# Moving two of nine depthwise taps onto TensorE, and the rest onto VectorE in half tiles, in the feed-forward stage of a four-layer convolution kernel

## The reference, cut to what matters

```
h   = relu(batchnorm1(c1 @ y))            384 channels, 48 x 48
g   = relu(batchnorm2(depthwise3x3(h)))   nine taps per channel, zero border
o   = c3 @ g + c3_b                       96 channels
s   = sigmoid(se2 @ relu(se1 @ mean(o)))
x   = x + o * (1 + s)
```

## Time and profile before

| | |
|---|---|
| median of 3 runs | 3150.25 us (3146.51 to 3150.44) |
| profiled execution | 3148.91 us, span of its instructions 3147.0 us |
| granted TensorE clock, mean | 0.89 of full |
| busy over the whole span | PE 2207.9 us (70%), DVE 2572.6 us (82%), ACT 1624.5 us (52%), POOL 2092.8 us (67%) |
| the changed stage, from the end of the last VectorE instruction before it to the end of its last | 2128.5 to 2322.9 us, 194.4 us |
| busy in that stretch | PE 130.29, DVE 151.95, ACT 86.20, POOL 85.14 us |

### The profile page before, as it was taken

The page is one execution under the profiler, slowest core; times in us unless marked ns, Lnnn a source line. Parts: engine busy times, 40 slices in busy tenths (PEclk is TensorE's granted clock), DMA queues, the critical chain, the costliest instruction groups (busy, mean ns, idle before and its releaser), DMA issues. The chain is left out here.

```text
span 3147.0 us, 24979 instructions
## 1 busy us (share of the span) xinstructions
PE 2207.9 (70%) x7334; PEld 1072.0 (34%) x7334; DVE 2572.6 (82%) x2080; ACT 1624.5 (52%) x2316; POOL 2092.8 (67%) x1126
## 2 busy tenths in 40 slices
PE   6754566677776676777666777789524989689389
PEld 3421233333333333333333333343112545355344
DVE  5556899999999999999999999956983656689630
ACT  2576577677677767777777677625410000263220
POOL 0154799999999999999999999933720000098000
PEclk9876799999999999999999999986666989799689
DMA  1274333333343333333343333250008888300360
GB/s 45 83 213 196 114 116 117 104 119 114 103 119 117 106 116 116 104 114 116 112 118 104 114 117 114 82 177 0 0 23 290 304 281 303 103 8 8 81 82 23
DMA packets 152198, 368.13 MB, mean 117 GB/s; under 512 B 54271, under 2 KB 69766, under 8 KB 140102
## 3 DMA queue, kind: packets, MB, share of 16 engines
q1 hardware_dynamic: 150852, 361.30, 37.3%
q10 hardware_dynamic: 1218, 5.31, 0.6%
HBM read 302.16 MB, written 51.00 MB: 112 GB/s over the span
## 5 line engine op out<-in xcount | busy, mean ns | idle before, releaser
L807 POOL TENSOR_TENSOR l0c_r<-l0c_r,l0c_v 128x768 f32<-128x768 f32 x576 | 1042.8, 1827 | 27.0 <-DVE l0c_r L770 26.5
L837 ACT ACTIVATE ps<-l0c_dlt,l0c_na 128x512 f32<-128x512 f32 (+1 forms) x1152 | 625.9, 575 | 520.0 <-DVE l0c_h L796 504.4
L816 POOL TENSOR_TENSOR l0c_hcp<-l0c_cb,l0c_h 128x768 f32<-128x768 f32 x384 | 701.9, 1828 | 1.5 <-DVE l0c_h L796 1.5
L796 DVE TENSOR_TENSOR_SCAN l0c_h<-ps,l0c_h,l0c_r 128x768 f32<-128x768 f32 x384 | 693.3, 1805 | 1.2 <-issue 1.2
L728 PE MATMUL ps<-l0c_hcp,net_ident 128*128 128x512 f32 (+1 forms) x1536 | 597.5, 514 | 14.1 <-ACT l_Z L830 7.3
L847 ACT ACTIVATE l0c_r<-l0c_S,l0c_floor,l0c_na 128x768 f32<-128x768 f32 x576 | 579.7, 1013 | 0.0
L695 PE MATMUL ps<-l0c_Bp,l0c_sel 96*128 96x512 bf16 (+1 forms) x1152 | 296.4, 340 | 381.8 <-DVE l0c_hcv L777 225.4
L770 DVE SCALAR_TENSOR_TENSOR l0c_r<-l0c_r,ps 128x768 f32<-128x768 f32 x576 | 533.8, 927 | 14.5 <-PE ps L695 9.4
L728 PEld LDWEIGHTS ps<-l0c_hcp,net_ident 128*128 128x128 f32 x1536 | 275.8, 200 | 269.4 <-issue 207.0
L1310 PE MATMUL ps<-l_prod,l_wa 128*96 128x384 f32 (+1 forms) x888 | 292.1, 493 | 85.2 <-DVE l_prod L1294 85.2
L796 DVE TENSOR_TENSOR_SCAN l0c_h<-ps,l0c_r 128x768 f32<-128x768 f32 x192 | 335.1, 1746 | 1.0
(11 more groups left out here) (274 smaller groups left out, 2530.9 us busy)
## 6 DMA issues: line engine op xcount, KB each, us to landing
l0c_cb<-cf SPq DMA_DIRECT2D x768, 192.0 KB, 3.3
l_other<-po SPq DMA_DIRECT2D x72, 1152.0 KB, 5.2
dlt<-l0s_dl SPq DMA_DIRECT2D x36, 384.0 KB, 2.3
v<-l0s_vv SPq DMA_DIRECT2D x36, 384.0 KB, 2.9
l0c_dlt<-dlt SPq DMA_DIRECT2D x36, 384.0 KB, 3.9
l0c_v<-v SPq DMA_DIRECT2D x36, 384.0 KB, 4.4
l0c_Bp<-bc SPq DMA_DIRECT2D x36, 144.0 KB, 4.0
l0c_Cp<-bc SPq DMA_DIRECT2D x36, 144.0 KB, 5.4
```

Of the source, the lines that this page charges most:

```text
L796: dve.tensor_tensor_scan(h[:, n, :], da[j % 2], r[:, j % NR, :], init, ALU.mult, ALU.add).then_inc(s_scan, 1)
L807: pool.tensor_tensor(r[:, j % NR, :], r[:, j % NR, :], v[:, (j // N) % 2, :], ALU.mult).then_inc(s_w, 1)
L816: pool.tensor_tensor(hcp[:, p % NHP, :], cb[:, p % NCB, :], h[:, e % N, :], ALU.mult).then_inc(s_hp, 1)
L837: act.activation(da[e % 2][:, part], dlt[:, i, part], ACT.Exp, scale=na[:, i, n:n + 1]).then_inc(done, 1)
```

## The change

The two sides of it are these:

- The first MM = 2 taps of every tile become products on TensorE: `diag[:, ot, i, :]` is a 128 x 128 matrix with the tap's weight of each channel on its diagonal, and the moving operand is the shifted window of `pad`. They sum in PSUM.
- The other OWN = 7 taps are all on VectorE, in half tiles of three chunks (128 x 1152). The first of the seven reads the PSUM sum as its addend, the others the accumulator.
- ScalarE's tap products and GpSimd's sums are gone. GpSimd makes the six diagonals at the start of the stage.
- The PSUM banks are dealt anew: three banks for each of two half tiles in turn (banks 0 to 5), and banks 6 and 7 in turn for all c1 and c3 chunks. The order on TensorE becomes: taps of half n, then three chunks of the next tile's c1 (for the last tile, of the first image's c3). On ScalarE: `finish` of half n - 1, then the three chunks of half n.
- `finish` and `t3` go by halves, with one `t3` buffer for each image (the first of them is the memory of Z), and c3 goes chunk by chunk for both images.
- Only the border of the `pad` buffers is cleared.

```diff
-        prod = sb("prod", [128, 2, L])
-        t3 = sb("t3", [128, OT, L])
+        acc = sb("acc", [128, 2, HB * CH])
+        diag = sb("diag", [128, OT, MM, 128])
+        t3 = (t3a, sb("t3", [128, OT, L]))
...
+            def free(r):
+
+                if r >= 2:
+                    if r - 2 < NJ * NC:
+                        pe.wait_ge(s_ev, r - 1)
+                    else:
+                        pe.wait_ge(s_o, r - 1 - NJ * NC)
+
+            def c1_chunk(j, c):
                 b, ot = tiles[j]
...
+                r = j * NC + c
+                free(r)
+                for f, (lo, hi, t) in enumerate(feeds[b]):
+                    mm = pe.matmul(ps[:, bank(6 + r % 2)], c1[lo:hi, t, ot * 128:(ot + 1) * 128],
+                                   U[lo:hi, t, c * CH:(c + 1) * CH], start=(f == 0), stop=(f == 1))
+                mm.then_inc(s_c1, 1)
+
+            def c3_chunk(b, c):
+                r = (NJ + b) * NC + c
+                free(r)
                 for ot in range(OT):
...
+                    pe.wait_ge(s_t3, 2 * (b * OT + ot) + (2 if c >= HB else 1))
+                    mm = pe.matmul(ps[0:C, bank(6 + r % 2)], c3[:, ot, :], t3[b][:, ot, c * CH:(c + 1) * CH],
+                                   start=(ot == 0), stop=(ot == OT - 1))
+                mm.then_inc(s_c3, 1)
+
+            def taps(n):
+                j, half = divmod(n, 2)
+                ot = tiles[j][1]
+                pe.wait_ge(s_diag, MM * (ot + 1))
+                pe.wait_ge(s_ev, NC * j + (NC if half else HB + 1))
+                if n >= 2:
+                    pe.wait_ge(s_tap, OWN * (n - 2) + 1)
+                for i in range(MM):
+                    dy, dx = divmod(i, 3)
+                    for c in range(HB):
+                        y0 = HR * half + 8 * c + dy
+                        mm = pe.matmul(ps[:, bank(HB * (n % 2) + c)], diag[:, ot, i, :],
+                                       pad[:, j % 3, y0:y0 + 8, dx:dx + W], start=(i == 0), stop=(i == MM - 1))
+                mm.then_inc(s_sum, 1)
+
+            for c in range(NC):
+                c1_chunk(0, c)
+            for n in range(2 * NJ):
+                j, half = divmod(n, 2)
+                taps(n)
+                for c in range(HB * half, HB * half + HB):
+                    if j + 1 < NJ:
+                        c1_chunk(j + 1, c)
+                    else:
+                        c3_chunk(0, c)
+            for c in range(NC):
+                c3_chunk(1, c)
...
+            for c in range(NC):
+                fill(0, c)
+            for n in range(2 * NJ):
+                j, half = divmod(n, 2)
+                if n:
+                    finish(n - 1)
+                for c in range(HB * half, HB * half + HB):
+                    if j + 1 < NJ:
+                        fill(j + 1, c)
+                    else:
+                        out(0, c)
+            for c in range(NC):
+                if c == HB:
+                    finish(2 * NJ - 1)
+                out(1, c)
...
-                dve.memset(pad[:, i, :, :], 0.0).then_inc(s_pad, 1)
+                dve.memset(pad[:, i, 0:PW:PW - 1, :], 0.0).then_inc(s_pad, 1)
+                dve.memset(pad[:, i, 1:1 + H, 0:PW:PW - 1], 0.0).then_inc(s_pad, 1)
...
+                dve.wait_ge(s_sum, n + 1)
+                if n >= 2:
+                    dve.wait_ge(s_t3, n - 1)
+                for k, i in enumerate(range(MM, TAPS)):
                     dy, dx = divmod(i, 3)
...
+                    if k:
+                        dve.wait_ge(s_tap, OWN * n + k)
+                    dve.scalar_tensor_tensor(
+                        dst, pad[:, j % 3, r0 + dy:r0 + dy + HR, dx:dx + W].rearrange("p (c h) w -> p c h w", h=8),
+                        c2[:, ot, i:i + 1], dst if k else total, ALU.mult, ALU.add).then_inc(s_tap, 1)
...
+            for ot in range(OT):
+                for i in range(MM):
+                    pool.tensor_scalar(diag[:, ot, i, :], ident[:, :], c2[:, ot, i:i + 1], None, ALU.mult
+                                       ).then_inc(s_diag, 1)
```

More of the change, by code:

```diff
@@ L1018, in _, with l0_ffn @@
                 pool.tensor_tensor(wa[:, i, 0:w, :], wa[:, i, 0:w, :], wb[:, i, 0:w, :], ALU.add).then_inc(s_pair, 1)
-def l0_ffn(nc, ps, X, U, acc, w):
+def l0_ffn(nc, ps, X, U, t3a, ident, w):
     OT = 2 * E // 128
[L1025 to L1028, removed]
+    NJ = B * OT
+    MM = 2
+    OWN = TAPS - MM
+    HB = NC // 2
+    HR = 8 * HB
     with ExitStack() as ctx:
@@ L1043, in l0_ffn @@
          ) = map(sem, "dve inv root bn pad c1 ev tap t3 c3 o m h s1 g e".split())
-        s_first, s_prod, s_sum = map(sem, "first prod sum".split())
+        s_diag, s_sum = map(sem, "diag sum".split())
         block = ctx.enter_context(nc.Block())
@@ L1049, in l0_ffn, with bank @@
         tiles = [(b, ot) for b in range(B) for ot in range(OT)]
+        def bank(i, n=CH):
+            return slice(i * BANK, i * BANK + n)
         @block.tensor
         def _(pe):
-            def c1_tile(j):
-                b, ot = tiles[j]
[L1055 to L1077, removed]
-                for ot in range(OT):
[L1079 to L1084, removed]
@@ L1094, in _ @@
             pe.wait_ge(s_s1, 1)
-            pe.matmul(ps[0:C, 7 * BANK:7 * BANK + B], se2[:, :], s1[:, :], start=True, stop=True).then_inc(s_g, 1)
+            pe.matmul(ps[0:C, bank(1, B)], se2[:, :], s1[:, :], start=True, stop=True).then_inc(s_g, 1)
         @block.scalar
@@ L1101, in _, with fill @@
             act.wait_ge(s_bn, 1)
-            act.wait_ge(s_pad, 3)
-            def stage(j):
+            act.wait_ge(s_pad, 6)
+            def fill(j, c):
                 b, ot = tiles[j]
[L1107 to L1122, removed]
@@ L1124, in finish @@
-            def finish(j):
-                b, ot = tiles[j]
[L1126 to L1148, removed]
+                r = j * NC + c
+                if j >= 3 and c == 0:
+                    act.wait_ge(s_tap, OWN * 2 * (j - 2))
+                act.wait_ge(s_c1, r + 1)
+                act.activation(pad[:, j % 3, 1 + 8 * c:9 + 8 * c, 1:1 + W],
+                               ps[:, bank(6 + r % 2)].rearrange("p (h w) -> p h w", w=W), ACT.Relu,
+                               scale=sc[:, 0, ot:ot + 1], bias=bi[:, 0, ot:ot + 1]).then_inc(s_ev, 1)
@@ new lines, in finish, with out @@
+            def finish(n):
+                j, half = divmod(n, 2)
+                b, ot = tiles[j]
+                act.wait_ge(s_tap, OWN * (n + 1))
+                act.activation(t3[b][:, ot, HB * CH * half:HB * CH * (half + 1)], acc[:, n % 2, :], ACT.Relu,
+                               scale=sc[:, 1, ot:ot + 1], bias=bi[:, 1, ot:ot + 1]).then_inc(s_t3, 1)
+            def out(b, c):
+                act.wait_ge(s_c3, b * NC + c + 1)
+                r = (NJ + b) * NC + c
+                act.activation(to[:, b, c * CH:(c + 1) * CH], ps[0:C, bank(6 + r % 2)], ACT.Identity,
+                               bias=c3b[:, :], accum_out=m[:, b, c:c + 1]).then_inc(s_o, 1)
```

42 lines of the change are left out of this document (12 added, 30 removed).

## The result

| | before | after |
|---|---|---|
| median of 4 runs | 3149.47 us (3146.51 to 3150.44) | 3117.83 us (3114.50 to 3120.79) |
| profiled execution, and its span | 3148.91 us, 3147.0 us | 3116.02 us, 3114.1 us |
| the stage: from the end of the last VectorE instruction before it to the end of the second update of X | 2128.48 to 2322.90: 194.42 us | 2129.26 to 2290.74: 161.48 us |
| of this: start, up to the first tap on VectorE | 22.49 us | 25.36 us |
| first tap to end of last tap on VectorE | 154.63 us | 120.68 us |

The ratio of the times is 0.9901 (95% interval 0.9884 to 0.9918). The profiled executions differ by 32.9 us, and so do the two stages; what stands before the stage took 0.8 us longer and what stands behind it 0.7 us less. The forecast was 3117.5 us, from a sum of -32.7.

What follows compares the result with a forecast made beforehand. VectorE, most busy but blocked by GpSimd's SBUF reads, was taken to bound the stage. Taps -34.2, start +3.3 and tail -1.8 sum to -32.7 us: 3116.2 profiled, 3117.5 as median; range 3109 to 3130.

Steps and rivals of the forecast that it cites:

- Taps: VectorE's first to last tap: twelve halves of 10.03 us make 120.4 us against 154.6, so -34.2 us.
- The estimate of 105.9 us: VectorE's 84 taps by the skill's fixed cost of 58 cycles, 14.5 us under the prediction's own sum; not adopted.
- something else slowed the taps: Rival: VectorE's taps stay slow because something other than GpSimd slowed them; chance almost nothing.
- Start: Stage start up to VectorE's first tap: twelve diagonal TensorE instructions come first, +3.3 us (bounds +1.1 and +4.9).
- the upper bound: In the start: if memsets cost as much as now, chunk 2 would be 4.5 us late.
- The loop: Halves of the stage: next taps ready in 7.7 of VectorE's 10.03 us, 2.3 spare, no cost at full clock.
- a pause of 2.5 us before a fall: Seen in the scan, clock falling to 0.57 after it; claimed that none of the loop's pauses is that long.
- a granted clock of 0.50 in any stretch of the loop: Sign in TensorE's profile that would show the prediction wrong; 1.00 was expected from about 2154 to 2280.
- Falling in every half: Rival: TensorE's clock falls in the loop's pause, at most every second half pays, 15 us: 3132; chance 0.08.
- Low throughout: Rival: TensorE stays at 1.2 GHz all through, about 100 us more: 3217; chance 0.05, including over five halves.
- Up early in tile 0's c1: Rival: TensorE's clock rises during tile 0's first chunks, some 10 us less: 3107.5; chance 0.05.
- Tail: From VectorE's last tap to the stage's end: 15.5 us against 17.3 now, -1.8 us.

Runs made afterwards that it cites:

- gp_off: The kernel before with GpSimd's sums and their ScalarE tap products moved to VectorE: stage 166.76 us against 194.4, total 3117.60 us in one run.
- gp_load: The changed kernel plus twelve needless GpSimd sums of 128 x 2304 on two buffers nothing else uses: stage 215.26 us, total 3170.91 us.
- memset_whole: The changed kernel with the padded buffers cleared whole instead of only their borders: stage 165.50 us against 161.5, total 3114.60 us.
- early: The changed kernel with the first taps after four chunks instead of six, all chunks two further ahead: stage 162.73 us, total 3115.62 us.
- rows_first: early with tile 0's six 128-row products made first, in a row into banks 0 to 5: stage 159.70 us, total 3111.22 us.
- mm1: The changed kernel with one tap of nine on TensorE instead of two, eight on VectorE: stage 177.33 us, total 3130.76 us.
- gp_off_again: The same kernel as gp_off, run again with five runs: stage 166.76 us, median 3121.36 us, ratio 0.9916 to the kernel before.

## Why the prediction was right

**Taps, -34.2 forecast, -33.95 measured.** A half takes 10.05 us, not 10.03. Durations taken from the one other place in the kernel with the same instruction were exact. The estimate of 105.9 us by the Trainium skill, "VectorE: DVE Perf Modes", section "The TRN2 errata", was 14.8 under the 120.7 measured.

**That GpSimd was the cause.** `gp_off` takes away the sums and the ScalarE products that feed them; `gp_load` adds sums without such products, and the taps stretch again, so it is GpSimd and not ScalarE. The rival that something else slowed the taps has fallen. The prediction said that time is lost "where both engines read SBUF at once"; `gp_load` sharpens this to a tap that stands still until the sum has ended.

**Start, +3.3 forecast, +2.9 measured.** The first burst took 5.89 us, not 6.2. The border clears cost next to nothing and delayed nothing; `memset_whole` gives 4.0 for the case that they had not been cut, where 4.5 was the upper bound.

**The loop.** TensorE's pause (1.07 against "about 1") and its work were as worked out, and no half waited. One sentence was wrong: it named a pause of 2.5 us before a fall and said that none of the loop's pauses is that long, as if that were enough. After one pause of 1.07 the clock did fall, in the second profiled execution of the changed kernel too. The prediction had named a granted clock of 0.50 in any stretch of the loop as a sign of being wrong; it came, for 3.4 us. It cost nothing, because 2.3 us were spare and 1.7 were used. That margin, and not the clock, carried the forecast: in `early` and `rows_first`, where the taps of a usual half are ready only 1.3 us ahead of VectorE, falls cost 1.5 to 2.8 us each.

**The rivals on the clock.** Falling in every half: no, once in twelve. Low throughout: no; the first diagonal burst lifted it. Up early in tile 0's c1: not in this kernel, where 19 us ran at 0.50; `rows_first` shows that this hangs on the order of the row counts. The Trainium skill, "TensorE: Matmul & The Clock Gate", Part 1, would have sustained activity release the throttle; these 19 us differ, and they decide. The Trainium skill's rule on depth-cycling, in the same page, shows in one fall here and in several in `mm1`, none of which costs time.

The kernel before has one more row on the order, which the prediction passed over. It read only that c1 stayed low after 50 us; the next window, under the weight loads of the change from the first image to the second, shows the rise, in the middle of the same unbroken burst:

```profile
2184.16 0.51 PEld L1059 LDWEIGHTS ps<-l_Y,l_c 64*128 64x128 f32 x4 [1.08 <-issue]
...
2185.00:2190.00 5.00, 5.00 (x15) 0.92 0.00 0
```

By windows of 0.2 us the clock rose there at 2185.8, 56.8 us after the burst began, and in `gp_off` and `gp_off_again` 56.7 us after it. Each time this is right behind the one place where two 64-row products (four weight loads) stand one behind the other. That fits the order as the cause; but the time since the start of the burst is the same in all three as well, and no run tried the break by itself.

**Tail, -1.8 forecast, -1.9 measured** (15.44 against 15.5): two chunks of c3 behind `finish` and the same gate as before.

**The total.** The three terms give -32.9 against a forecast of -32.7. That the median came within 0.4 us of the forecast is luck beyond that: the four runs of the changed kernel lie 6.3 us apart, and the medians differ by 31.6.

What the prediction didn't see is how the gain is made up. It booked the taps on TensorE and the taps freed of GpSimd as one sum. Taken apart, 27.7 us are GpSimd's absence and 5.3 all the rest: VectorE's work falls from 126.7 to 120.7, 6.1 us, the tail loses 2.1, and the start gives 2.9 back.

## What to carry to other kernels

When one instruction's longest duration is nearly three times its shortest, look at what the neighbouring engine has in work before you give it a share: here "help" that took over 13 of 48 taps made the stage 28 us longer. After such a change, look for what the new bound leaves idle: one microsecond a half on TensorE and a start at half clock were worth 14 us more. Work moved ahead at a queue's front comes out at its end, so count the tail with it.

## What the runs showed of the hardware

- A VectorE instruction with both tensors in SBUF that begins beside a GpSimd sum stands still for all that is left of the sum: 1.42 us became 4.87 and 6.08 (`gp_load`). One already in work when the sum began kept its 1.42. With one of the two tensors in PSUM it ran in 1.42 beside the sum.
- Float32 products that alternate between 128 and 64 rows left TensorE at 1.2 GHz for 19 us, and in the kernel before for 56.8, until two 64-row products followed each other; twelve of 128 rows alone took 6.76 to 6.92 us and ended at 2.4 GHz, in four kernels. Once up, the same alternation kept the level, in `gp_off` for 29 us. Why this is so was not tried further.
- Pauses of 0.86 to 1.07 us in the changed kernel's loop were followed by a fall of the clock once in seven, in its second execution once in six, and in `memset_whole`, which has the same loop, in none of eight. In `mm1` all nine pauses of 1.31 us and more were. What decides it for the short ones stays open.
